# A graph network's first two node stages hand one of their matrix products to the edge pass that follows, and ScalarE's eviction takes over the maximum with zero

## The reference, cut to what matters

```
x = features; outs = []
for l in range(3):
    h = x @ fc_w[l].T + fc_b[l]
    f = einsum(h * norm_out, ch_w[l])               # four channels of 64
    m = f[src] * edge_w
    agg = segment_sum(m, dst)
    x = relu(agg * norm_in + ch_b[l])
    outs.append(x)
return concatenate(outs) @ mlp_w.T + mlp_b
```

## Time and profile before

| what | value |
|---|---|
| time, median of 3 runs | 5877.78 us (5876.99 to 5884.57) |
| time of the profiled execution | 5887.29 us |
| its span, first to last instruction | 5885.6 us |
| mean granted TensorE clock | 0.657 of full |
| busy, share of the span | PE 47%, DVE 56%, ACT 17%, POOL 55% |
| DMA, mean over the span | 151 GB/s |
| stage n1 | about 743 to 839 us of the span |
| pass e1, first to last gather | 839.8 to 1467.5 us |
| stage n2 | about 1497 to 1593 us |
| pass e2, first to last gather | 1593.3 to 2220.5 us |
| stage n3 | about 2250 to 2326 us |

### The profile page before, as it was taken

The page is one execution under the profiler, slowest core; times in us unless marked ns, Lnnn a source line. Parts: engine busy times, 40 slices in busy tenths (PEclk is TensorE's granted clock), DMA queues, the critical chain, the costliest instruction groups (busy, mean ns, idle before and its releaser), DMA issues. The chain is left out here.

```text
span 5885.6 us, 44062 instructions
## 1 busy us (share of the span) xinstructions
PE 2776.5 (47%) x11716; PEld 2005.1 (34%) x11716; DVE 3271.0 (56%) x9305; ACT 1027.7 (17%) x2639; POOL 3238.8 (55%) x3351
## 2 busy tenths in 40 slices
PE   5111053444633446454442000387676776677675
PEld 4110042222422224221121000365555654466554
DVE  5577444444544445477775777655554555445454
ACT  3223323333333333100002111110001000010002
POOL 4556635655255553566635666246663666546662
PEclk8555575555755556676666555688778877788786
DMA  3445524444244442355534665235553555435552
GB/s 107 158 159 178 181 96 156 161 157 168 91 148 164 160 157 75 113 171 176 173 114 130 193 192 188 90 121 179 177 176 103 169 182 176 154 112 189 172 183 86
DMA packets 270426, 887.64 MB, mean 151 GB/s; under 512 B 69115, under 2 KB 108904, under 8 KB 227048
## 3 DMA queue, kind: packets, MB, share of 16 engines
q0 software_dynamic: 157728, 428.39, 24.9%
q1 hardware_dynamic: 112456, 456.51, 20.1%
HBM read 438.85 MB, written 445.80 MB: 150 GB/s over the span
## 5 line engine op out<-in xcount | busy, mean ns | idle before, releaser
L1325 POOL DMA_INDIRECT WORK<-table,SRCI x1376 | 1320.1, 959 | 1043.2 <-issue 467.8
L1325 POOL DMA_INDIRECT WORK<-table,BYSRC x1092 | 1067.6, 978 | 840.5 <-issue 542.7
L1351 PE MATMUL e_pm<-ARENA 128*128 128x256 f32 (+1 forms) x4200 | 1110.5, 416 | 311.0 <-issue 306.6
L1351 PEld LDWEIGHTS e_pm<-ARENA 128*128 128x128 f32 (+1 forms) x4200 | 860.5, 209 | 539.7 <-issue 423.7
L1407 DVE SCALAR_TENSOR_TENSOR WORK<-WORK,NST,e_mv 128x256 f32<-128x256 f32 x1173 | 562.6, 480 | 544.8 <-issue 360.3
L1407 DVE SCALAR_TENSOR_TENSOR WORK<-WORK,LOWE 128x256 f32<-128x256 f32 x1288 | 626.7, 487 | 95.4 <-remote 27.6
L1372 ACT ACTIVATE e_mv<-WORK,WE 128x256 f32<-128x256 f32 x1176 | 486.0, 458 | 327.0 <-DVE WORK L1407 255.4
L1753 POOL DMA_INDIRECT WORK<-table_attention,SRCI x392 | 374.5, 955 | 195.6 <-issue 119.4
L902 PE MATMUL e_rb<-ARENA 98*128 98x128 bf16 x392 | 114.5, 292 | 756.6 <-ACT ARENA L918 676.7
L1407 DVE SCALAR_TENSOR_TENSOR WORK<-WORK,LOWE,e_pm 128x256 f32<-128x256 f32 x84 | 40.4, 480 | 712.3 <-PE e_pm L1351 344.3
L902 PEld LDWEIGHTS e_rb<-ARENA 98*128 98x128 bf16 x392 | 95.6, 244 | 774.7 <-ACT ARENA L918 686.5
(11 more groups left out here) (384 smaller groups left out, 5332.4 us busy)
## 6 DMA issues: line engine op xcount, KB each, us to landing
edge_results<-WORK SPq DMA_DIRECT2D x336, 1024.0 KB
edge_results_attention<-WORK SPq DMA_DIRECT2D x98, 544.0 KB
WORK<-table,SRCI POOLq DMA_INDIRECT x1376
table<-ARENA SPq DMA_DIRECT2D x29, 640.0 KB, 3.2
WORK<-table,BYSRC POOLq DMA_INDIRECT x1092
WORK<-table_attention,SRCI POOLq DMA_INDIRECT x392
edge_results<-WORK SPq DMA_DIRECT2D x7, 512.0 KB
edge_results<-WORK SPq DMA_DIRECT2D x28, 128.0 KB
```

The costliest lines, as they stand in the source:

```text
L1325: eng.indirect_dma_start(slot(g, k), None, T, bass.IndirectOffsetOnAxis(ap=index[:, t:t + 1], axis=0)).then_inc(landed, 16)
L1351: last = eng.matmul(made_ps[:, i % 4, 0:D], hot_rows[0:n, i % 2, j, :], AGG[0:n, j, :], start=j == 0, stop=j == NT - 1)
```

## The change: what it does

In n1 and n2 the second product, its addition to X and the `w2` columns in PSUM are gone. SP writes each turned tile XT to a new DRAM tensor HT, 128 KB a tile, and ACT waits before it overwrites a slot of XT (5 slots) until that write has landed. In the following pass, e1 or e2, `mlp_beside` runs beside `rank_beside`: at group 3t SP reads tile t of HT into one of two buffers, at group 3t + 1 PE multiplies it with that third of `mlp_w` into a PSUM bank of its own, at group 3t + 2 DVE adds the product to X. In all three node stages the scaled sum goes straight to R, and the maximum with zero is taken by ACT's eviction of the turned tile (Relu in place of Copy).

```diff
+        HTT = sb("HTT", [P, 2, D])
+        HT = dram("turned_layers", [NP, D])
...
@@ node_products, ACT @@
                         eng.wait_ge(made_free, t + 1)
-                        eng.activation(C[:, t, 0:D] if keep_turned else XT[:, slot, :], tps[:, t % 2, 0:D], ACT.Copy).then_inc(xt, 1)
+                        if kept and t >= u:
+                            eng.wait_ge(kept[slot], t // u * 16)
+                        eng.activation(C[:, t, 0:D] if keep_turned else XT[:, slot, :], tps[:, t % 2, 0:D],
+                                       ACT.Copy if stage is None else ACT.Relu).then_inc(xt, 1)
@@ node_products, SP @@
+                        def keep_turned_tile(t):
+                            eng.wait_ge(xt, t + (u + 1))
+                            eng.dma_start(keep_rows[t * P:(t + 1) * P, :], XT[:, t % u, :]).then_inc(kept[t % u], 16)
+
                         for at in CHUNKS:
+                            if kept:
+                                for t in range(min(at.start + 3, NT) if at.start else 0, min(at.stop + 3, NT)):
+                                    keep_turned_tile(t)
                             eng.wait_ge(done, u + at.stop)
...
+                        for sem in kept:
+                            eng.wait_ge(sem, NT // u * 16)
                         eng.wait_ge(stored, len(CHUNKS) * 16 * len(tables))
@@ stage_gcn @@
-                eng.scalar_tensor_tensor(TMP2[:, slot, :], tile_of(AGG, t), norm_in[:, ds(t, 1)], CHB[:, layer, :],
-                                         ALU.mult, ALU.add).then_inc(chain, 1)
-                eng.wait_ge(chain, t + 1)
-                eng.tensor_scalar(R[:, slot, :], TMP2[:, slot, :], 0.0, None, ALU.max).then_inc(staged, 1)
+                eng.scalar_tensor_tensor(R[:, slot, :], tile_of(AGG, t), norm_in[:, ds(t, 1)], CHB[:, layer, :],
+                                         ALU.mult, ALU.add).then_inc(staged, 1)
@@ gcn_table, out2 @@
-                eng.tensor_tensor(tile_of(X, t), ps[:, D:2 * D], tile_of(X, t), ALU.add)
@@ mlp_beside(w), new @@
+                def at(phase, fn):
+                    def step(g, q, turn):
+                        if g % 3 == phase and g // 3 < NT:
+                            fn(g // 3)
+                    return step
+                def on_sync(eng):
+                    def fetch(t):
+                        if t >= 2:
+                            eng.wait_ge(made, t - 1)
+                        eng.dma_start(HTT[:, t % 2, :], HT[t * P:(t + 1) * P, :]).then_inc(read[t % 2], 16)
+                    return [], [(at(0, fetch), 0)]
+                def on_tensor(eng):
+                    def multiply(t):
+                        eng.wait_ge(read[t % 2], (t // 2 + 1) * 16)
+                        if t:
+                            eng.wait_ge(moved, t)
+                        for k in range(2):
+                            last = eng.matmul(own[:, 0:D], HTT[:, t % 2, k * P:(k + 1) * P], w[:, k, :], start=k == 0, stop=k == 1)
+                        last.then_inc(made, 1)
+                    return [], [(at(1, multiply), 0)]
+                def on_vector(eng):
+                    def add(t):
+                        eng.wait_ge(made, t + 1)
+                        eng.tensor_tensor(tile_of(X, t), own[:, 0:D], tile_of(X, t), ALU.add).then_inc(moved, 1)
+                    return [], [(at(2, add), 0)]
@@ flow_l0 @@
-                edge_pass(f"e{l}", SRCI, (ALU.mult, ALU.add), NST, True, rank_beside(l) if l else numbers_and_weights_beside)
+                edge_pass(f"e{l}", SRCI, (ALU.mult, ALU.add), NST, True, all_beside(rank_beside(l), mlp_beside(MW[:, l - 1])) if l else numbers_and_weights_beside)
...
-                    node_products(f"n{l + 1}", stage_gcn(l), GW[:, l + 1], out1, MW[:, l], out2,
-                                  gather=(PR, end_sum), table=(AGG, T), crossing=0)
+                    node_products(f"n{l + 1}", stage_gcn(l), GW[:, l + 1], out1, None, out2,
+                                  gather=(PR, end_sum), table=(AGG, T), crossing=0, keep_rows=HT)
```

More of the change, by code:

```diff
@@ L1013, in node_products @@
         def node_products(name, stage, w1, out1, w2=None, out2=None, gather=None, table=None, table2=None, scatter=None, marks=None,
-                          norm=None, crossing=None, keep_turned=False):
+                          norm=None, crossing=None, keep_turned=False, keep_rows=None):
             n2 = 0 if w2 is None else w2.shape[2]
@@ L1028, in node_products @@
                 got = gathered[0:NT // u]
+                kept = [] if keep_rows is None else [st.sem(f"kept{k}") for k in range(u)]
                 if norm is not None:
@@ L1115, in ahead @@
                         eng.wait_ge(turned, t + 1)
-                        stage(eng, t, slot, chain, staged)
+                        stage(eng, t, slot, staged)
                     def behind(t, slot, _):
@@ L1228, in stage_gcn, with stage @@
         def stage_gcn(layer):
-            def stage(eng, t, slot, chain, staged):
-                eng.scalar_tensor_tensor(TMP2[:, slot, :], tile_of(AGG, t), norm_in[:, ds(t, 1)], CHB[:, layer, :],
-                                         ALU.mult, ALU.add).then_inc(chain, 1)
-                eng.wait_ge(chain, t + 1)
-                eng.tensor_scalar(R[:, slot, :], TMP2[:, slot, :], 0.0, None, ALU.max).then_inc(staged, 1)
+            def stage(eng, t, slot, staged):
+                eng.scalar_tensor_tensor(R[:, slot, :], tile_of(AGG, t), norm_in[:, ds(t, 1)], CHB[:, layer, :],
+                                         ALU.mult, ALU.add).then_inc(staged, 1)
             return stage
@@ L1639, in all_beside, with mlp_beside, beside @@
             return beside
+        def mlp_beside(w):
+            def beside(st, name):
+                made, moved = st.sem("mlp_made"), st.sem("mlp_moved")
+                read = [st.sem(f"mlp_read{k}") for k in range(2)]
+                own = st.stack.enter_context(nc.psum_tensor(f"{name}_mlp", [P, 512], F32))
+                def at(phase, fn):
[23 more added lines that the diff above has]
+                    return [], [(at(2, add), 0)]
+                return dict(sync=on_sync, tensor=on_tensor, vector=on_vector)
+            return beside
         def own_term_beside(w, bias=None):
```

## The result

| | kernel before | changed kernel |
|---|---|---|
| median, first comparison | 5881.17 us (5876.99 to 5893.15, 4 runs) | 5830.74 us (5809.34 to 5836.29, 4 runs) |
| profiled execution, its span | 5887.29, 5885.6 | 5833.67, 5831.9 |
| granted clock, mean | 0.657 | 0.657 |

The ratio on record is 0.9899 (0.987 to 0.9928). It is not the ratio of the two medians, which is 0.9914: the medians differ by 50.4 us, the ratio says 59, and 35.2 was forecast. The sign was right, the size was not. A gain in e1 and e2, which is where the difference lies, had been given 5%, by another course of events.

What follows compares the result with a forecast made beforehand. The prediction held n1's steady half bound by PE, n3's by a loop of DVE, PE and ACT, and e1 by no one engine's work. Terms -18.3 - 17.9 - 3.0 + 4 = -35.2 took 5877.8 to 5843 us, range 5828 to 5885.

Steps and rivals of the forecast that it cites:

- The second product leaves: n1 and n2: loop at 1.78 us a tile without the second product, saving 18.3 and 17.9 us.
- the rival of a falling clock: n1 and n2: PE's clock falls with less work, 16 us more in each stage; 5910 us, 2%.
- The maximum moves, in n3 too: n3: with the maximum on ACT the loop takes 1.72 us a tile for 1.86, saving 3.0 us.
- Relu for Copy costs nothing: Node stages: ACT's eviction takes no longer with Relu; maximum left on DVE would make the saving 9 us less.
- The writes cost nothing: n1 and n2: the 25 writes of 128 KB are out in time, cost taken as 0.
- I take 4 us for both passes: e1 and e2: added products, additions and reads mostly lie off the path, costing 4 us, between 0 and 17.
- it is issued one group ahead of its use, a group is 6.5 us: e1 and e2: SP's read, an estimated 4.3 us behind a 1 MB store, has 6.5 us before its use.
- The first rival: e1 and e2: a product breaks gather bursts, each extra pause costing 6.3 us; 5940 us, 11%.
- Faster yet: e1 and e2: shorter bursts bring the passes nearer POOL's own pace, 19 us off one pass; 5824 us, 5%.
- e1's gathers from first to last 628 us as before: e1: sign that the forecast is right, the gathers' span unchanged at 628 us.
- The likeliest case: Whole kernel: the forecast itself, 5843 us, with its own range of 5832 to 5856; 63%.

Runs made afterwards that it cites:

- group 5: Last follow-up runs, h1 to h4, on one chip with pauses, the kernel before timed beside them: ratios 0.993, 0.9918, 0.9984 and 0.995.
- d2: Changed kernel with the maximum put back on VectorE; ratio 0.9928 to the kernel before.
- d3: Changed kernel without the products beside e1 and e2 and without the writes feeding them, first two layers' last-weights product omitted; ratio 0.9912 to the kernel before.
- h1: Changed kernel with each turned tile's read beside e1 and e2 issued one product earlier; 5834.37 us, ratio 0.993 to the kernel before.
- h4: Changed kernel with the products beside e1 and e2 begun at group 6 of the gathers, not 0; ratio 0.995 to the kernel before.
- h3: The kernel before itself, unaltered, run for a second profile; ratio 0.9984 to the kernel before.
- h2: The changed kernel itself, unaltered, beside its variants on one chip; 5822.45 us, ratio 0.9918 to the kernel before.
- d4: Changed kernel with the products beside e1 and e2 begun at group 21 of the gathers, not 0; ratio 0.9964 to the kernel before.
- f4: Changed kernel with POOL allowed four groups ahead of ScalarE's moves, in e1 and e2 in place of six; ratio 0.9912 to the kernel before.
- f1: Kernel before with a POOL wait added at gather group 12 of e1 and e2; 5842.99 for 5860.50 us, ratio 0.9968.
- f3: Changed kernel, POOL waiting at gather group 13 of e1 and e2 until one more group is moved; ratio 0.994 to the kernel before.
- group 4: Follow-up runs f1 to f4, waits added to POOL, on one chip with pauses: ratios 0.9968, 0.9949, 0.994 and 0.9912 to the kernel before.
- f2: Changed kernel, POOL waiting at gather group 14 of e1 and e2 until two more groups are moved; ratio 0.9949 to the kernel before.
- c3: Kernel before with a POOL wait added at gather group 12 of e1 and e2, on the chip without pauses; ratio 1.0001.

## Why the prediction was wrong, point by point

1. **The second product leaves: right.** Forecast 18.3 and 17.9 us, the moved maximum of n1 and n2 counted in, measured 19.0 and 18.2 on the first chip (16.5 and 17.9 in group 5, 19.0 and 19.1 on the chip without pauses). n3's loop of the earlier trace rows foretold the new pace of 1.78 us a tile within 0.03. PE's clock stayed high (0.90), so the rival of a falling clock is out.
2. **The maximum moves, in n3 too: right**, -3.4 us for -3.0; d2 gives it 2.9.
3. **Relu for Copy costs nothing: right.** Put back on VectorE (d2) it costs 9.2 us in the three stages by the table, and the forecast had 9. The rule of the Trainium skill, "ScalarE: Activation LUTs", section "Rules for kernel authors", that relu belongs on VectorE does not hold where ScalarE evicts the tile anyway, 128x256 in f32 here: the runs decide for ScalarE.
4. **The writes cost nothing: right** (d3).
5. **This step failed.** "I take 4 us for both passes" was written as a price on a pass whose rhythm stays. As a price it was fair, if anything high: with the rhythm held (h1 and h4 against h3) products, reads and additions cost 0.9 to 1.8 us a pass, hardly more than the 1.4 and 1.5 by which two profiles of the kernel before differ. But "it is issued one group ahead of its use, a group is 6.5 us" was wrong: in h2 PE was free for the second product at 883.35 - 3.39 = 879.96, only 1.4 us behind the read's issue at 878.52, and the product began 4.8 us behind that issue. The forecast's own 4.3 us for the store ahead was more than that 1.4. A group ahead in the lists is not a group ahead in time: SP's read stood behind a store that waits for DVE's sums (L1419) of the same group, and PE's product and the meeting ahead of it don't wait for those. So the second product was late by 3.4 us; TensorE's transposes and ScalarE's take came late with it; POOL made one short pause more at group 12, and every later pause moved by two groups. The pass then ended with two takes in its tail and not three. The term is -5.2 and -4.5 us, not +2 and +2, which is 13.7 of the 15.1 us missed; the rest is items 1 and 2. In e1 the -5.2 is -8.0 in the tail and +2.8 in the gathers, about the one pause more.

A reading in the same item was also too sure: the earlier trace rows put DVE's 154.5 us down to "issue" and its 144.9 to "remote", that is, to nothing the profile names, and I called them waits for ACT and for PE.

The first rival had the mechanism in hand, a product between a meeting and a turning that splits a burst, and asked only what an extra pause costs (6.3 us, where the one that came lasts 3.0). It didn't ask where the pauses then fall at the end of the pass. "Faster yet" had the sign, but its reason, shorter bursts nearer to POOL's pace, is not what happened: from first to last gather e1 grew by 2.8 us. And "e1's gathers from first to last 628 us as before" was a bad test, since the gain lies behind the last gather.

The range, 5828 to 5885, held the median of 5830.74 by 3 us, but not the change by the recorded ratio: 5877.8 x 0.9899 is 5818 us. The likeliest case's own range, 5832 to 5856, missed both, since its +4 had bounds of 0 and 17, without a gain. (Its upper end is also added up wrongly: 5843 + 13, without the 6 us that 0.15 us more in 42 tiles would give.) I had a reason to bound it at 0 only for the work, not for the order of pauses.

Open: the tail goes with the place of the last pause in every profile that has pauses, 30.1 to 30.4 us behind 94 and 21.9 to 22.1 behind 96, at POOL's lead of six groups, whatever moved it there (d4's 33.5 and 35.1 have products in them; f4 has a lead of four). What comes before the tail is less clear. From first to last gather f1 took 620.8 and 619.3 us and f3 624.4 and 622.6, where the other profiles with pauses have 625.6 to 632.0, so the early pauses count as well, and no run separates those. No version was shown to beat the changed kernel, and group 4 couldn't show it, since the changed kernel was not timed in it: f4's whole, 0.9912 (0.9877 to 0.9947), is not apart from f2's 0.9949 (0.9929 to 0.997).

## What to carry to other kernels

Where engines run in bursts, ask of an added operation not only what it costs but where it moves the rhythm, and count what is left over at the end of the loop: here a late read of 128 KB was worth 5 us a pass, in the good direction, and issuing the reads earlier lost them. Such a gain is no property of the change, so it should be read from stage lengths and reported by itself: what the change gives by construction is the 40.6 us of the node stages. And a transfer's slack is to be read from the timeline, from its issue to the moment its user is free, and not from the mean length of a step.

## What the runs showed of the hardware that I had not expected

**A chip without the pauses.** The kernel before took 5860 to 5885 us in the first comparison and in three of the four later groups (three chips), and 4763 in the other. The mean granted clock differs little, 0.695 (c3) for 0.657. Of the 154 us between the two in e1, 142.8 are POOL's pauses and 19.6 the tail (10.5 us for 30.1), less 8.6 by which the gathers without the pauses took longer there. The node stages differ too: n1 took 73.0 us there (c3) and 96.1 on the first chip. A gather itself takes the same 0.95 us, 1.25 us apart, on both. Whether this belongs to the chip, or to something that changed between the groups, no run shows; each group ran on a chip of its own.

**ScalarE's waits for TensorE end late while POOL issues gathers.** On the chips with pauses, ScalarE's take is released long after the transposes that it waits for. In the first profile of the kernel before, the last transpose for the take of the earlier trace rows ended at 1093.58, the take began at 1105.34, 2.9 us after POOL's last gather of that burst; the profile calls it "remote", since nothing recorded ends at that moment. Takes that fall soon behind a restart of POOL start at once: h2's transpose ended at 887.23 (886.94 and 0.29), its take began at 887.26, with POOL back at its gathers since 877.91. The two instructions of the kernel before, beside those of the earlier trace rows:

```profile
1093.29 0.29 PE L893 MATMUL e_rt<-identb,ARENA 128*32 128x128 bf16 x1
...
1101.48 0.95 POOL L1325 DMA_INDIRECT WORK<-table,SRCI  x1 [0.30 <-issue]
```

On the chip without pauses e1's takes waited 9.1 us in all for the transposes. What holds the signal back no run here shows. Every "remote" wait on an engine that waits for TensorE beside a burst of gathers should be read with that in mind, and two chips compared before a stage is called bound by anything.
